# Hybrid transformer, last gated layers: chosen rows added to the output by indirect transfers instead of a product with a 0/1 matrix, with a new order of the steps

## The reference

```python
x = x + attn_a(layernorm(x))   # layer 0: causal attention, 16 heads of 16, rotary positions
x = x + ffn(layernorm(x))      # layer 1: gated
x = x + attn_b(layernorm(x))   # layer 2: full attention, 16 heads of 64, relative bias
x = x + ffn(layernorm(x))      # layer 3: gated, same weights as layer 1

def ffn(t):                    # (B, N, D), C = N // 2
    gate = sigmoid((t @ Wg)[..., 0])
    _, idx = top_k(gate, C)                       # the 256 tokens with the largest gates
    a = take_along_axis(t, idx[..., None], axis=1)
    o = attention_16_heads(a @ Wq, a @ Wk, a @ Wv) @ Wo
    gate_sel = take_along_axis(gate, idx, axis=1)
    return zeros_like(t).at[arange(B)[:, None], idx].set(o * gate_sel[..., None])
```

## Time and profile before

| | |
|---|---|
| median of 3 runs | 2024.09 us (2023.55 to 2024.71) |
| profiled execution | 2022.95 us |
| its span, first to last instruction | 2020.9 us |
| PE busy | 1970.7 us (98%) |
| DVE busy | 1518.8 us (75%) |
| ScalarE busy | 1158.5 us (57%) |
| GpSimd busy | 690.7 us (34%) |
| DMA | 102.42 MB, mean 51 GB/s |
| granted TensorE clock | 0.998 |

### The profile page before, as it was taken

How to read it: one execution, slowest core, us unless ns; L and a number is a source line. 1 busy time by engine, 2 the same in 40 slices (tenths; PEclk the granted TensorE clock), 3 DMA queues, 4 the chain that set the end, 5 groups by cost and what they waited for, 6 DMA issues and landing times.

```text
span 2020.9 us, 41852 instructions
## 1 busy us (share of the span) xinstructions
PE 1970.7 (98%) x15934; PEld 1264.9 (63%) x15934; DVE 1518.8 (75%) x4803; ACT 1158.5 (57%) x2578; POOL 690.7 (34%) x879
## 2 busy tenths in 40 slices
PE   8999999999999999999999999999999999999998
PEld 6566665666665666656666566655666566666577
DVE  8987767767877778868779687796787967856536
ACT  2455674575637765376644757367663576627642
POOL 5323234242333323433324324234233342313320
PEclk9999999999999999999999999999999999999999
DMA  4001221111201121111211112011120111102200
GB/s 170 2 1 35 78 79 46 46 54 35 84 27 54 46 73 46 45 36 63 74 37 35 54 46 83 29 53 54 42 78 19 61 54 41 68 16 72 76 6 11
DMA packets 31078, 102.42 MB, mean 51 GB/s; under 512 B 3105, under 2 KB 11425, under 8 KB 30753
## 3 DMA queue, kind: packets, MB, share of 16 engines
q1 hardware_dynamic: 30880, 99.76, 14.9%
HBM read 95.56 MB, written 4.19 MB: 49 GB/s over the span
## 4 chain that ended last, share of the span: by engine, by line
PE 76%; DVE 19%; ACT 3%; issue 1%; POOL 0%; DVEq 0%
PE ps L959 21%; PE ps L1711 11%; PE ps L1693 11%; PE ps L1701 9%; PE ps L1472 6%; DVE ps L1327 5%; PE ps L1555 3%; PE ps L1660 3%; PE ps L1569 3%; PE ps L1648 3%; DVE probs L1418 2%; PE ps L1626 2%; PE ps L1531 2%; DVE peaks L1401 1%; DVE stats L1247 1%
## 5 line engine op out<-in xcount | busy, mean ns | idle before, releaser
L1132 POOL TENSOR_SCALAR probs<-probs,rtotal 128x512 f32<-128x512 f32 x512 | 353.7, 709 | 651.3 <-DVE rtotal L1427 650.5
L1223 ACT ACTIVATE probs<-probs,peak 128x512 f32<-128x512 f32 x512 | 365.3, 714 | 152.5 <-DVE peak L1423 152.3
L1418 DVE CUSTOM_DVE_ANT_0 probs<-ps,band 128x512 f32<-128x512 f32 x512 | 332.7, 687 | 70.7 <-PE ps L1693 70.1
L1232 ACT ACTIVATE PT<-ps 128x512 f32<-128x512 f32 x512 | 266.5, 620 | 56.7 <-PE ps L1701 55.4
L1701 PEld LDWEIGHTS ps<-ident,probs 128*128 128x128 f32 x2048 | 225.7, 141 | 48.9 <-issue 38.9
L1701 PE MATMUL ps<-ident,probs 128*128 128x128 f32 x2048 | 249.9, 274 | 3.5 <-DVE peaks L1327 2.8
L1327 DVE CUSTOM_DVE_ANT_0 ps<-ps,later 128x512 f32<-128x512 f32 (+3 forms) x512 | 232.8, 525 | 13.6 <-PE ps L1531 12.7
L1693 PE MATMUL ps<-KT,QT 64*128 64x512 f32 x1024 | 242.2, 606 | 0.4
L1711 PE MATMUL ps<-PT,Vb 128*64 128x512 f32 x1024 | 237.1, 600 | 0.0
L959 PE MATMUL ps<-xnT,wb 128*128 128x512 f32 x512 | 234.8, 601 | 2.4 <-DVE peak L1418 1.7
L1196 ACT ACTIVATE PTc<-ps 128x384 f32<-128x384 f32 (+1 forms) x384 | 168.8, 553 | 70.0 <-PE ps L1555 69.4
(11 more groups left out here) (156 smaller groups left out, 3302.5 us busy)
## 6 DMA issues: line engine op xcount, KB each, us to landing
band<-in_band SPq DMA_DIRECT2D x64, 896.0 KB, 4.6
wb<-in_w_b SPq DMA_DIRECT2D x64, 384.0 KB, 3.1
x<-in_x SPq DMA_DIRECT2D x16, 256.0 KB, 3.1
out<-x SPq DMA_DIRECT2D x16, 256.0 KB, 2.2
cos<-in_cos SPq DMA_DIRECT2D x8, 256.0 KB, 2.7
sin<-in_sin SPq DMA_DIRECT2D x8, 256.0 KB, 3.0
wob<-in_wo_b SPq DMA_DIRECT2D x1, 1024.0 KB, 9.1
wqk<-in_wqk_a SPq DMA_DIRECT2D x1, 512.0 KB, 5.6
```

Of the source, the lines that this page charges most:

```text
L1132: last = g.tensor_scalar(unit, unit, rtotal[:, r % 8, e:e + 1], 1.0, ALU.mult, ALU.mult)
L1223: last = a.activation(unit, unit, ACT.Exp, bias=peak[:, r % 8, e:e + 1], accum_out=total[:, r % 8, e:e + 1])
L1232: a.activation(PT[:, k % 2, e, :, tile_of(q)], bank(now, name).rearrange("p (k n) -> p k n", k=NT), ACT.Copy).then_inc(act_read, 1)
L1418: v.tensor_tensor_reduce(out=probs[:, (r + LENT) % ROWS_HELD, e, :], in0=bank(now, name), in1=band[:, k % 2, e, lo:lo + T], scale=1.0, sca ...
```

## The change

In layer 3 (l == 3) only:

- f_spread is replaced by f_idx: 8 products in float32 of pick with `marks`, a matrix of two columns per token tile: the token's number and its gate. Slot by slot this gives the chosen token's number and gate. DVE adds T*s and writes the number as a 32-bit integer (`token`), and copies the gate (`gate_sel`).
- f_o is replaced by f_sc: the same product with Wo, and ScalarE scales each of the two tiles by gate_sel into `of`, in float32.
- f_y is replaced by f_add on POOL: two indirect transfers with addition, each of 128 rows of 1 KB, from `of` to the output rows in HBM that `token` names.
- x is stored at b_y, that is before layer 3 of the sequence, without the addition; f_add waits for these stores. The load of x for sequence s+3 stands at f_rank and waits for the normalisation and the stores. `c_ln` of s+3 follows f_ln of s in place of the last f_y.
- f_gather of a later layer waits for the indirect transfers out of the buffer it overwrites, and SP waits at the end for all of them.
- gate moves into column 1 of marks, with two more constants made on POOL (CONSTS 8 to 10).
- All numbers of PLACE are new, those of the steps of all layers.

Layer 1 keeps f_spread, f_o and f_y.

```diff
-CONSTS = 8
+CONSTS = 10
+    "f_idx": [("o", "dve", 1)], "f_sc": [("o", "act", 1)],
+    "added": {"f_add": 1},
+    "f_idx": [("pe", 0.6), ("dve", 0.15), ("dve", 0.15)],
+    "f_sc": [("pe", 1.729), ("act", 0.35), ("act", 0.35)],
+    "f_add": [("pool", 1.3), ("pool", 1.3)],
...
-    ("last1", "f_gather"): [22421],
-    ("last1", "f_q"): [21077],
+    ("last1", "f_gather"): [21071],
+    ("last1", "f_idx"): [23654],
+    ("last1", "f_k"): [20837],
+    ("last1", "f_q"): [21529],
...
-    late = [Step("f_y", s - 3, 3, 1)] if s >= 3 else []
+    late = [Step("f_ln", s - HELD, 3)] if s >= HELD else []
...
-           (f("part"), [f("ln")], []), (f("spread"), [f("rank")], []), (f("gather"), [f("rank"), f("part")], [])]
+           (f("part"), [f("ln")], []), (f("idx" if l == 3 else "spread"), [f("rank")], []), (f("gather"), [f("rank"), f("part")], [])]
...
+    if l == 3:
+        return out + [(f("sc"), [f("vb", 0), f("vb", 1), f("idx")], []), (f("add"), [f("sc")], [])]
...
+        out_rows = out.rearrange("b t d -> (b t) d")
...
-                        if kind == "f_y" and l == 3:
+                        if kind == "b_y" and q == 1:
                             sp.wait_ge(dve_read, plan.unit(now, now))
                             two = slice(2 * n, 2 * n + 2)
                             sp.dma_start(ov[s][:, two], x[:, s % HELD, two]).then_inc(x_stored[s % HELD], 16)
-                            if n == 1:
-                                sp.wait_ge(x_stored[s % HELD], 32 * (s // HELD + 1))
-                                if s + HELD < B:
-                                    load_x(sp, s + HELD)
+                        if kind == "f_rank" and l == 3 and s + HELD < B:
+                            sp.wait_ge(xn_done, plan.after("xn", Step("f_ln", s, l), now))
+                            sp.wait_ge(x_stored[s % HELD], 32 * (s // HELD + 1))
+                            load_x(sp, s + HELD)
+                    sp.wait_ge(out_added, 32 * B)
...
+                    for some in marks:
+                        g.iota(some[:, :, 0], pattern=[[P, NT]], base=0, channel_multiplier=1,
                                allow_small_or_imprecise_dtypes=True).then_inc(consts, 1)
...
+                        if kind == "f_add":
+                            pool.wait_ge(x_stored[s % HELD], 32 * (s // HELD + 1))
+                            pool.wait_ge(dve_read, plan.unit(Step("f_idx", s, l), now))
+                            pool.wait_ge(act_read, plan.unit(Step("f_sc", s, l), now))
+                            for j in range(NS):
+                                g.indirect_dma_start(out_rows, bass.IndirectOffsetOnAxis(m.token[:, j:j + 1], 0), m.of[:, j, :], None,
+                                                     bounds_check=B * T - 1, compute_op=ALU.add).then_inc(out_added, 16)
...
+                        if kind == "f_sc":
+                            act.wait_ge(dve_read, plan.unit(Step("f_idx", s, l), now))
+                            for j in range(NS):
+                                last = a.activation(m.of[:, j, :], bank(now)[:, j * D:(j + 1) * D], ACT.Copy,
+                                                    scale=m.gate_sel[:, j:j + 1])
+                            last.then_inc(act_read, 1)
                         if kind == "f_gather":
+                            old = plan.latest(now, "f_add")
+                            if old is not None:
+                                at_least(act, out_added, 32 * plan.after("added", old, now))
...
+                        if kind == "f_idx":
+                            found = bank(now)[:, 0:2 * NS].rearrange("p (j k) -> p j k", k=2)
+                            v.tensor_scalar(m.token, found[:, :, 0], float(T * s), None, ALU.add)
+                            v.tensor_copy(m.gate_sel, found[:, :, 1]).then_inc(dve_read, 1)
...
+                        if kind == "f_idx":
+                            at_least(pe, consts, CONSTS)
+                            pe.wait_ge(pick_done, plan.after("pick", Step("f_rank", s, l), now))
+                            room(now)
+                            for j in range(NS):
+                                last = product(o[:, 2 * j:2 * j + 2], [(m.pick[:, t, tile_of(j)].bitcast(F32), m.marks[:, t, :])
+                                                                       for t in range(NT)])
-                        if kind == "f_o":
+                        if kind in ("f_o", "f_sc"):
```

More of the change, by code:

```diff
@@ new lines @@
+    ("cycle", "f_part"): [-402],
+    ("cycle", "f_q"): [208],
+    ("cycle", "f_rank"): [-49],
+    ("cycle", "f_row"): [-88],
+    ("cycle", "f_rq"): [174],
+    ("cycle", "f_spread"): [93],
+    ("cycle", "f_v"): [208],
+    ("cycle", "f_va"): [407, 442],
+    ("cycle", "f_vb"): [-404, -1129],
+    ("cycle", "f_xq"): [225],
+    ("cycle", "f_y"): [582, -41],
+    ("cycle3", "f_add"): [5238],
+    ("cycle3", "f_gate"): [4779],
+    ("cycle3", "f_gather"): [4914],
+    ("cycle3", "f_hk"): [2217],
@@ new lines @@
+    ("first1", "f_ln"): [-430],
+    ("first1", "f_m"): [781, 928],
+    ("first1", "f_o"): [1226],
+    ("first1", "f_p1"): [451, 769, 670, 771],
+    ("first1", "f_p2"): [920, 845, 116, -366],
+    ("first1", "f_part"): [-1122],
+    ("first1", "f_q"): [356],
+    ("first1", "f_rank"): [269],
+    ("first1", "f_row"): [256],
+    ("first1", "f_rq"): [-1034],
+    ("first1", "f_spread"): [1035],
+    ("first1", "f_v"): [356],
+    ("first1", "f_va"): [957, 1008],
+    ("first1", "f_vb"): [-1561, 943],
```

437 lines of the change are left out of this document (205 added, 232 removed).

## The result

Before, the median is 2024.18 us (8 runs beside the changed kernel); after, it is 2030.94 us (2028.28 to 2032.26, 8 runs). The ratio is 1.0033, with a 95% interval of 1.0022 to 1.0044: slower, where 2015.2 us and "faster" had been forecast. The profiled execution took 2031.01 us with a span of 2029.3, against 2022.95 and 2020.9 before, so 8.4 us of span have to be found.

A forecast was written before the change was run, and what follows sets the result against it. PE, busy 237.9 of 242.1 us per period, was taken as the bound. PE -4.9, DVE -3.5 and the end -0.45 sum to -8.85: median 2015.2 us, range from 2 us below Rival (a)'s 2006.0 up to 2034.

The forecast's parts named there:

- f_idx, 1.73 us: PE's index product per last gated layer: 16 records at 0.108 us; net gain 0.70 per layer, 4.9 us over seven.
- Rival (a): Cheap indices: f_idx records go at 0.026 us, seven layers give 14.1 us instead of 4.9; 2006.0 us, chance 0.14.
- DVE's relief, -3.5 us: VectorE does 3.4 us less per period; 0.5 of it was taken to shorten PE's waits, times 7.
- The order, 0 and at most 1 us per sequence: All place numbers are new; taken as 0, with 1 us per sequence either way, 8 us.
- Rival (c): The new order eats the gain: 1 us more waiting per sequence, 2023.2 us, no change; chance 0.15.
- POOL, nothing: f_add's two indirect transfers per layer, 1.2 us per issue, fit into POOL's idle hole of 10.33 us; no cost.
- rival (b): f_add delays row normalisations that b_tr waits for, slack 0.62 us; 2027.7, 2035.6 or 2042.7 us, slower; chance 0.19.
- ScalarE, SP and CONSTS, nothing: Scaled copies (0.2 us more), moved stores and loads on SP's queue, and more iotas were to cost nothing.
- The end, -0.45 us: Behind the last f_o: copies, two issues of 1.2 us, landing 3.1; -0.45 us, between -2.4 and +2.9.
- f_idx in the tail, nothing: In the last sequence f_idx falls into PE's wait before the scores, costing nothing; ahead of the gather 0.4 to 2.0 us.
- Rival (d), a better packed opening: A fifth of the opening's 40.5 us of filling transposes goes: 8.1 us less, 2007.1 us, chance 0.09.

The follow-up runs named there:

- e2: The kernel before (old code) with the changed kernel's place numbers; 2035.93 us, ratio 1.0059.
- e12: e10 with the index product as one fp32r pass on four columns, the gate split behind f_row's comparisons; 2020.24 us, ratio 0.9984 to the kernel before.
- e1: The changed code with the place numbers of the kernel before; 2034.2 us, ratio 1.0056 to the kernel before.
- e4: The changed kernel without its indirect transfers, so layer 3's gated rows never reach the output; 2022.39 us, ratio 0.9992 to the kernel before.
- e9: e7 with the planner's TensorE price of f_idx at 1.71 us instead of 0.6, resizing only filling transposes; 2027.8 us, ratio 1.0017 to the kernel before.
- e10: e9 with 32 opening place numbers chosen anew so TensorE is planned never to stand over 0.8 us; 2025.94 us, ratio 1.0007 to the kernel before.
- e5: The changed kernel with the opening's place numbers (first, first0, first1) of the kernel before; 2030.95 us, ratio 1.0042 to the kernel before.
- e7: The changed kernel with f_rq and f_xq ahead of f_idx in the last sequence; 2029.05 us, ratio 1.003 to the kernel before.
- e6: The kernel before without the 32 filling transposes at 99.62 us; 2023.51 us, ratio 1.000.
- e3: The changed kernel with 26 more identity transposes issued before f_row of sequence 0, layer 1; 2029.11 us, ratio 1.0026 to the kernel before.
- e14: The changed code in the old order (e1) without the six filling transposes ahead of layer 1's gate row; 2033.17 us, ratio 1.0057 to the kernel before.
- e8: Meant to remove e1's six filling transposes, but a wrong row name left them in, so the same program as e1; 2034.38 us.
- e13: e12 with the opening's and period's order chosen anew from measured durations, without the opening's pause; 2012.14 us, ratio 0.9949 to the kernel before.

## Why the prediction was wrong, step by step

- **f_idx, 1.73 us.** Right: 1.70 in the period. The transposes of the earlier trace rows were the right neighbour. Within the new order the new code gives 0.5 per period (e2), where 0.70 and VectorE's 0.5 had been added, and in the old order it costs 0.9 (e1). The product's price follows its records (e12). Rival (a) is out.
- **DVE's relief, -3.5 us.** Wrong; it was a choice without a row. VectorE's busy time fell by 3.8 us per period, and TensorE's waits on it still come to 2.8 us. The same two names lead them, gX and peaks, 1.1 and 0.6 to 0.7 us: less work elsewhere on VectorE did not shorten them. That they are latencies of one operation after another is my reading. That f_y's products were cover for a row of probabilities (e1) was missed as well; there the removed 1.99 us was worth about 1.1.
- **The order, 0 and at most 1 us per sequence.** This is the step that failed, and with it the rule that TensorE work taken out comes off the span nearly one for one. Both rest on the new code keeping the cover that the old order gave. The period grew by 0.4 us where it was to fall by 1.2: TensorE's busy time fell by 0.5, its waits for VectorE stayed, and its other waits grew. Neither half alone does better (0.9 us lost per period in e1 and in e2). Up to the last b_y of s=1 5.5 us are lost, and I had given the opening no loss at all; e2, with the old code, loses 5.3 there. Rival (c) had the mechanism in the periods, 8 us in all; I gave it 0.15. The clock I had read as 1.00 in the period and as 0.98 in the earlier trace rows, and made nothing of it.
- **POOL, nothing.** Right in the periods (e4): 1.6 us per issue instead of 1.2, and yet no wait, so rival (b) is out. GpSimd did come onto the path at another place, the low halves, by half a microsecond and through the order.
- **ScalarE, SP and CONSTS, nothing.** No row speaks against it: ScalarE is busy 144.8 us in a period in both kernels.
- **The end, -0.45 us.** Measured +0.65, within the bounds of -2.4 to +2.9, but by other parts. The copies ended at 2022.3, where the forecast's distance put them. Then 0.9 us pass before GpSimd issues, each issue takes 1.6 us in place of 1.2, with 0.3 between the two, together 1.9 more; and the last transfer lands 2.2 us after its issue ended, where I had put 3.1. The Trainium skill gives about 2.0 us fixed for such a DMA (DMA: Bandwidth & Descriptors, the section on the anatomy of a DMA on the SWDGE path). Counted behind the issue, as the prediction used it, the 2.2 us agree with that; from the start of the issue it is 3.7.
- **f_idx in the tail, nothing.** Wrong, 1.0 us. I placed it in TensorE's wait and did not ask what stands behind its two reads in VectorE's queue, nor whether the filler around it was sized for it. The place is bad for the old code too: in e2 the two comparisons of f_spread, 1.40 us, stand ahead of the combination, and from the last b_y to f_o it is 46.7 us.
- **Rival (d), a better packed opening.** The fillers in the first 200 us are 280 records now, not fewer, and TensorE stops 2.94 us between them.
- **Rival (b)** has 2027.7 and 2035.6, and 2030.94 lies between them. That is luck: its mechanism, GpSimd's transfers holding up b_tr, is not there (e4).

In numbers, the forecast -8.85 us against +8.4: up to 594 us +5.5, of which e2, with the old code, shows 5.3; in the six sequences behind it +1.2 measured (1.6-0.4) where 6 x 1.2 were to be won; +1.0 ahead of f_o and +0.7 behind it. That most of the 5.5 is the clock is likely and not proven: 4.8 us lie between e9's runs and no such stretch is in e10, but the order of e10's opening differs too, and e5 loses most of the time without a low clock.

## What to carry to other kernels

When a change comes with a new order of work, price the order as a term of its own and with both signs: ask which operation the old order hid behind the removed one, and test the two halves apart. A planner keeps the promises of its price table only: measure every new operation and write its duration into the table before the order is chosen, fillers included. In a kernel bound by TensorE, look at its longest pause in every stretch that is not full; the granted clock behind it can cost more than the pause.

## What the runs showed of the hardware

- In the profiled executions with a pause of TensorE of 2.9 us at 105 us, the granted clock stood at the 1.2 GHz level for 13.7 to 20.5 us (the changed kernel 20.5, e2 and e4 17.1, e7 and e9 13.7). After e6's pause of 4.3 us it was 10.2 us. In e3, 2.8 us of pause and 26 transposes behind it, it was 6.8. Where the longest pause there was 1.7 us it was none (e1, e5, e14), 3.4 us (before) or 6.8 (e8, the same program as e1), and in e10 to e13, with no pause over 1.1 us behind 50 us, none.
- An indirect, adding transfer of 128 rows holds GpSimd 1552 to 1791 ns, the next one starts 0.3 us later, and it lands 3.6 to 7.3 us after its issue began, 3.9 in the median. The first of a pair lands after 3.8 to 4.0 us, the second of a pair within the periods after 6.7 to 7.3, and in the last two pairs after 3.7; the very last is 2.2 us after its issue ended.
- A product with float32 weights of 128x128 goes at 0.106 us per record with two moving columns, near the 0.108 with 128 in the earlier trace rows, and leaves two records; as fp32r it leaves one.
- Two operations of VectorE on 8 and 4 columns took 1.2 us each beside GpSimd's subtractions, and 0.16 and 0.17 away from them.
- Two subtractions of GpSimd of 128x512 take 2.51 us together, 2.95 when a gX of VectorE (1.28 us) that is already running has 0.6 us left, and 3.45 when it has 1.1 left. Where they start first they keep their 2.52 us and gX takes 1.84 (e13).
